# A decoder block on one core: VectorE adds the experts' second result and the first projection at later places in its program

## What is computed

```python
x = x + attn(layernorm(x), Wqkv, Wo, bo)              # 16 heads of 64, 8 pooled "agent" tokens
x = x + xattn(layernorm(x), ctx, ctx, Wq, Wk, Wv, Wo)  # 16 heads of 8, causal
x = x + ffn(layernorm(x), ...)                         # gate picks 2 of 16 experts, 2 shared experts
# xattn
scores = einsum('bhqd,bhkd->bhqk', Q, K) / sqrt(8) + causal
heads  = einsum('bhqk,bhkd->bhqd', softmax(scores), V)
out    = heads @ Wo.T
# ffn
h  = silu(x @ We1 + be1) * (x @ We3 + be3)
y  = sum over experts of combine * (h @ We2 + be2)
z  = silu(x @ ws1 + bs1) * (x @ ws3 + bs3) @ ws2 + bs2
out = y + z
```

## Time and profile before

| | |
|---|---|
| median of 3 runs | 1147.37 us (1146.27 to 1149.27) |
| the profiled execution | 1149.95 us |
| its span, first to last instruction | 1148.2 us |
| mean granted TensorE clock | 0.932 |
| busy: TensorE, VectorE, ScalarE, GpSimd | 969.1, 787.1, 574.9, 227.4 us |

### The profile page before, as it was taken

How to read it: one execution, slowest core, us unless ns; L and a number is a source line. 1 busy time by engine, 2 the same in 40 slices (tenths; PEclk the granted TensorE clock), 3 DMA queues, 4 the chain that set the end, 5 groups by cost and what they waited for, 6 DMA issues and landing times.

```text
span 1148.2 us, 22137 instructions
## 1 busy us (share of the span) xinstructions
PE 969.1 (84%) x9069; PEld 768.3 (67%) x9069; DVE 787.1 (69%) x1841; ACT 574.9 (50%) x1148; POOL 227.4 (20%) x220
## 2 busy tenths in 40 slices
PE   6665899969997799978999799977999689986687
PEld 5553688747785587846886487856787477864566
DVE  3255966787866967678667878678666867669444
ACT  4433755366534665356554575346652675435322
POOL 6001420035000520014100340014200340004100
PEclk9886999989999899989999799999999899998789
DMA  5300010000100010000100000000100000000000
GB/s 146 80 1 1 2 38 1 10 10 2 37 11 10 1 39 1 11 10 2 37 11 1 10 17 23 10 11 2 38 1 10 11 2 1 10 2 10 1 1 19
DMA packets 28902, 18.36 MB, mean 16 GB/s; under 512 B 7649, under 2 KB 27394, under 8 KB 28802
## 3 DMA queue, kind: packets, MB, share of 16 engines
q1 hardware_dynamic: 26914, 12.48, 4.2%
q0 software_dynamic: 1280, 4.20, 1.2%
q10 hardware_dynamic: 608, 0.27, 0.1%
HBM read 12.62 MB, written 4.19 MB: 15 GB/s over the span
## 4 chain that ended last, share of the span: by engine, by line
PE 59%; DVE 21%; ACT 12%; issue 3%; POOL 3%; SPq 1%; DMA 0%; DVEq 0%; POOLq 0%
PE banks L510 8%; PE banks L491 5%; PE banks L674 5%; PE banks L493 4%; PE banks L492 4%; PE banks L624 3%; PE banks L606 3%; ACT M L870 3%; PE banks L648 3%; DVE sil L1171 3%; PE banks L769 3%; ACT PXUT L933 2%; PE banks L598 2%; PE banks L541 2%; PE banks L635 2%
## 5 line engine op out<-in xcount | busy, mean ns | idle before, releaser
L877 ACT ACTIVATE sil<-banks,b 128x512 f32<-128x512 f32 x144 | 99.4, 691 | 204.8 <-PE banks L493 202.5
L870 ACT COPY M<-banks 128x512 f32<-128x512 f32 x208 | 122.8, 608 | 87.0 <-PE banks L624 68.7
L510 PEld LDWEIGHTS banks<-w,hT 128*128 128x128 f32 x1152 | 152.9, 195 | 13.4 <-issue 6.1
L510 PE MATMUL banks<-w,hT 128*128 128x128 f32 x1152 | 156.0, 279 | 1.4 <-DVE hT L1178 1.4
L1171 DVE SCALAR_TENSOR_TENSOR sil<-banks,b,sil 128x512 f32<-128x512 f32 x128 | 95.7, 748 | 84.0 <-ACT sil L877 82.3
L389 POOL DMA_DIRECT2D out_x<-xn x16 | 12.9, 809 | 544.8 <-DVE xn L1184 544.8
L1178 DVE TENSOR_TENSOR hT<-sil,banks 128x512 f32<-128x512 f32 x128 | 87.8, 686 | 25.2 <-PE banks L500 21.3
L426 POOL TENSOR_TENSOR PXUT<-PXUT,rx 128x512 f32<-128x512 f32 x80 | 87.1, 1115 | 88.5 <-DVE rx L1240 88.5
L624 PE MATMUL banks<-ident,PXUT 128*128 128x128 f32 x384 | 63.0, 304 | 30.6 <-ACT M L870 26.9
L598 PE MATMUL banks<-maskb,pick 32*64 32x512 bf16 x512 | 39.8, 499 | 52.2 <-ACT PXUT L933 42.1
L624 PEld LDWEIGHTS banks<-ident,PXUT 128*128 128x128 f32 x384 | 44.8, 152 | 52.0 <-ACT M L870 37.8
(11 more groups left out here) (199 smaller groups left out, 2078.3 us busy)
## 6 DMA issues: line engine op xcount, KB each, us to landing
xin<-in_x SPq DMA_DIRECT2D x8, 512.0 KB, 4.1
cin<-in_ctx SPq DMA_DIRECT2D x8, 512.0 KB, 5.3
out_x<-xn POOLq DMA_DIRECT2D x16, 256.0 KB, 2.8
KQ<-in_L_attn_Wqkv SPq DMA_DIRECT2D x3, 512.0 KB, 5.2
KQ<-in_L_ffn_We SPq DMA_DIRECT2D x2, 512.0 KB, 4.6
KQ<-in_L_attn_Wo SPq DMA_DIRECT2D x1, 512.0 KB, 7.9
w<-in_L_ffn_We SPq DMA_DIRECT2D x1, 512.0 KB
woM<-xwT SPq DMA_DIRECT2D x16, 8.0 KB, 1.8
```

What stands on the lines that cost most here:

```text
L510: mm(ps(name)[:, P * t:P * t + P], hT[:, k % 2, P * t:P * t + P], w2[:, pair[k], :], start=(n == 0 and t == 0), stop=False, skip_group_che ...
L870: cp(dst, ps(name)[:] if src is None else src).then_inc(ready, 1)
L877: nc.scalar.activation(sil[:, k % 2, :], ps(f"H1_{k}")[:], ACT.Silu, bias=b1[:, pair[k]:pair[k] + 1]).then_inc(sil_ready, 1)
```

## The change

In the loop over the four steps, VectorE's second result of group e moves from behind the maxima and the expert unit of step 0 to behind the maxima of step 1. The addition of group g's first projection moves from between the maxima of step 3 and the sums of step 2 to behind those sums.

```diff
@@ -1345,11 +1345,12 @@
                         maxima(g, u)
                         if u == 0:
                             hidden(e, 17)
-                            result(e, 1)
                         else:
+                            if u == 1:
+                                result(e, 1)
+                            inverses(g, u - 1)
                             if u == UX - 1:
                                 add_x(g, 0)
-                            inverses(g, u - 1)
```

## The result

| | before | after |
|---|---|---|
| median of 4 runs | 1146.82 us (1145.11 to 1149.27) | 1115.25 us (1112.20 to 1116.66) |
| ratio, with its 95% interval | | 0.972 (0.969 to 0.9749) |
| profiled execution, its span | 1149.95, 1148.2 us | 1116.46, 1114.7 us |
| mean granted TensorE clock | 0.932 | 0.956 |

The change makes the kernel 2.8% faster, 31.6 us by the medians. The forecast was 23.1 us and 1124.3 us, with a range down to 1116: the direction was right and each edit removed the wait that it was to remove, but the sum held nothing for what TensorE's clock did ahead of the first projection. The gain was 8.5 us short, and the time fell just under the range.

The account below looks back on a forecast made before the run. No engine was taken to bound the kernel throughout; VectorE was the one waited for around both waits. First edit 15.1 plus second edit 8.0 gave 23.1 us off the 1147.37 us median: 1124.3 us, range 1116 to 1135.

Parts of the forecast that it names:

- What bounds it: Whole kernel: no engine bounds it throughout; around the two waits in steps 0 to 3, VectorE is the engine waited for.
- The store: GpSimd's store behind the second result: its 0.79 us still fit before the first reciprocals, costed at nothing.
- First edit: Second result behind step 1's maxima: its wait goes in seven expert stages, 15.1 us gained, ends 14.1 and 20.1.
- 4 x 2.02 + 3 x 2.33: Sum for the moved result: 2.02 us gained in four stages, 2.33 us in three with the longer wait, 15.1 us.
- Does it last: Steps 1 to 3: VectorE stays later than TensorE, 0.6 us to spare; 8.1 us instead of 7.5 between steps 1 and 2.
- Second edit: First projection's addition behind step 2's sums: 0.75 us in each of 7 groups, 2.7 in the last, 8.0 us; ends 0 and 17.6.
- The clock: TensorE's granted clock behind the gate: largest unknown, a spell worth at most 1.7 us; between -8.5 and +3.4 us.
- (a): Only the first edit pays, as ScalarE's copies and the ring of transposes set the stretch's second half: 1132.3 us, chance 0.10.
- (b): GpSimd's store is held by a pair of VectorE's reductions, 0.3 us lost in seven stages: 1126.4 us, chance 0.05.
- (d): No change: an engine that these waits don't reach sets each group's length, 1147.4 us, chance 0.05.
- (e): Slower: GpSimd isn't free again when its store is issued, delaying step 3 in seven stages; up to 1152.6 us, chance 0.03.
- (c): Everything waited for at both places is gained, 20.1 + 17.6 = 37.7 us: 1109.7 us, chance 0.03.

Follow-up runs that it names:

- e1: Only the second result moved behind step 1's maxima, against the kernel before: median 1127.19 us, ratio 0.9806.
- e3: The kernel before with 12 extra matmuls in TensorE's idle time ahead of step 2's scores: median 1151.61 us, ratio 1.004.
- e10: The kernel of e1 with 6 extra matmuls between step 0's values and step 1's transposes, in seven groups: median 1133.85 us, ratio 0.9899 to the kernel before.
- e2: Only the first projection's addition moved behind step 2's sums, against the kernel before: median 1135.21 us, ratio 0.988.
- e5: The kernel before with 8, 14 and 5 extra matmuls ahead of step 1's scores, step 2's scores and step 0's transposes: median 1150.54 us, ratio 0.9997.
- e7: The changed kernel with extra matmuls ahead of step 1's scores, step 0's transposes and in the last group: median 1106.33 us, ratio 0.9633 to the kernel before.
- e4: The changed kernel with 8, 2 and 6 extra matmuls ahead of step 1's scores, step 2's scores and step 0's transposes: median 1114.71 us, ratio 0.9702 to the kernel before.

## Why the prediction was wrong in size

**What bounds it**: right. VectorE is the later engine in steps 1 to 3, and both waits went without a new one in their place. The store, put at nothing, cost nothing.

**First edit, 15.1 us**: measured 16.5. In the three groups without a spell around step 1's scores in either profile, steps 0 to 2 fall from 16.35 to 14.30 us, 2.05 (forecast 2.02). The rest is that spell: the three groups that had it became 2.4 to 3.6 us shorter (forecast 2.33), and one that hadn't had it had it afterwards and gained only 0.76. The step "4 x 2.02 + 3 x 2.33" took the places of the spells as fixed.

**Does it last**: the 8.1 us between steps 1 and 2 came out at 8.06.

**Second edit, 8.0 us**: measured 11.5, and here the prediction failed. Its working for the edit itself holds: in the first group, at full clock before and after, 21.48 became 20.70 us, 0.78 (forecast 0.75), and between e1 at full clock and the changed kernel it is 0.77. What failed is the step that took TensorE's place from the row: "so the scores for step 3 are no later against VectorE than today", and from there the second projection 12.0 - 0.75 us behind step 3's maxima. In the row read, TensorE was at half clock, and the sum put an earlier arrival of TensorE's at nothing. Afterwards five of the seven groups with experts were clear, and four of these take 20.7 us instead of 22.4 to 22.9 (the fifth 21.9, the clock having fallen behind the transposes). In three of the four, step 1's transposes came 1.37 us earlier, and ScalarE's copies, its exponentials and both projections with them; in the fourth, clear before too, the first projection no longer ran at half clock. It is e1, the first edit alone, that shows this (6.1 us in a stretch that it doesn't touch), and the first groups of e3 and e10 that a spell by itself lengthens the stretch (1.64 and 1.08 us). In the last group the forecast was 2.7 us: e2 has 2.85, the changed kernel 1.9, since its transposes of step 1 came late.

**The clock**: named as the largest unknown, but only behind the gate, where the row stands at 0.83 and 1.00. There it gave 3.0 us of the 8.5 that were allowed for, as a spell costs 1.0 us and not the 1.7 taken as its most. In steps 2 and 3 the rows held it too (2.33 us for scores that the first group does in 1.23), and no bound was put on it.

**The range**: its low end, 1116, was the forecast less the gate's spells. It had no term for the clock of steps 2 and 3, where the rows would have allowed up to 7 x 1.37 = 9.6 us and 3.5 came beyond the forecast; with the gate's 3.0 and the first edit's 1.4 that is most of the 8.5.

**Rivals**: (a), (b), (d) and (e) are out. (c) gave 1109.7 and came nearer to the time (5.6 us) than the forecast (9.1), by luck: not every wait was gained, other time was. The additions' waits fell by 9.9 us, and the second edit was worth 0.78 a group, not the 2.37 of the wait.

**What stays open**: which idle time of TensorE's sets the clock of steps 2 and 3 and behind the gate. That the first edit goes with more clear groups and the second with fewer spells behind the gate stands in the counts above, e10 apart, and that a group with a spell in steps 2 and 3 is 0.9 to 1.8 us longer. Filling the idle time in the kernel before didn't bring clear groups about (e3, e5), so that it is the shorter idle time ahead of step 2's scores remains argued.

## What to carry to other kernels

A duration of TensorE's that is read from one row is a duration at that row's clock: look for the same instruction in another group (here 1.23 and 2.33 us) before taking it as the length of the work, and put the difference, times the groups, into the bounds of every stretch whose idle time the change alters. A wait that is removed on the engine that others wait for also moves their idle time, and TensorE's clock can change with it in stretches that the edit doesn't touch (e1: 6.1 us beside its own 16.5). Where TensorE idles ahead of work on the path, matmuls on constants into a free bank can be worth 9 us (e7, half of it in the last group's gate), but they gave nothing in e3 and e5, where the spell came all the same, and took 2.3 us in e4's first group, where they weren't done when the work was ready.

## What the runs showed of the hardware

The granted clock goes between its two levels, 2.4 and 1.2 GHz (1.00 and 0.50 in the rows), in spells that change place between two executions of the same program: five and seven of seven groups behind the gate in two profiles of the kernel before, two and one in the changed kernel. There TensorE was busy for the whole 10 us of the window in both kinds of group, at 0.83 and 1.00, so a spell also comes where TensorE shows no idle time, and costs 1.0 us of 58 there. In steps 2 and 3 the same 32 matmuls of the scores take 1.23 us at full clock and up to 2.33 with a spell, and one spell makes the stretch from step 3 to the fourth addition 1.64 us longer with the same program on VectorE (e3's first group). The Trainium skill (TensorE: Matmul & The Clock Gate, Part 1) says that the clock is gated by how busy TensorE has lately been; e7 agrees in the last group, where 22 matmuls ahead of the gate (21 in the trace) brought its matmuls from 3.59 to 2.02 us, and e3 shows that matmuls added at one place can leave the spell to come at the next.
